# Row maxima a batch and a half ahead of the scores in two attention layers, and merged output rows in the first

## The chip, the cores and the metric

The kernel runs on one core of a Trainium2 chip. The metric is the device time of one execution in microseconds (us).

## The reference

A transformer block pair on 16 batches of 256 rows of 256 features, all float32, with a fixed context `ctx_1024` of the same shape. Attention has 16 heads of 16 features, the first one without projections, the second with them:

```python
x = x + attn0(layernorm(x), ctx, ctx)          # softmax(q k^T / 4) v, 16 heads
x = x + moe(layernorm(x))                      # 8 experts, top 2 of the gate's logits, gelu
x = x + attn1(ctx=ctx, q_in=layernorm(x))      # q = w_q x, k,v = w_kv ctx, softmax, w_out, b_out
x = x + ffn(layernorm(x))                      # relu, float_quantize to (4,3), second matmul
```

A layernorm is `(x - mean) / sqrt(var + 1e-5)` over the features. The softmax is over the 256 context rows of a batch.

## The kernel before, in words

Four phases follow one another: the first attention (about 0 to 289 us of the profiled span), routing and experts (to about 832 us), the second attention (to about 1150 us) and the last feed forward. The change touches only the two attentions, `first_attention` (L123 to L693) and `second_attention` (to L1568). Each engine has its own instruction stream, with a loop over bodies b, one for each batch and a few more at both ends, and within a body eight steps g, one for each pair of heads. All order is written out by hand: in each stream `body(b)` names the step g at which a piece of work stands, and for which batch (`has(b + k)` is true where that batch exists).

For a batch and a pair g the work is:

- **Row maximum**, M(g) below: TensorE multiplies 128 queries with 256 keys, four matmuls (`row_max`, L404), into a big PSUM bank. VectorE reduces it to the negated maximum of each row, R(g) below (`reduce`, L603), and this frees the bank. When all eight pairs are reduced, TensorE turns the maxima (`turn_neg`, L437), ScalarE copies them (`neg_out`, L547) and the SP queue writes them as one more row into `q_stack` (`stack_neg`, L270).
- **Score**, S(g) below: the same product the other way round, with the negated maximum in it (`score`, L415), into the next big bank. ScalarE takes the exponential (`exp`, L535), which frees the bank.
- **Probabilities by values**: `pv` (L428), 16 matmuls for four heads, into a spare bank, and `pv_out` on ScalarE (L541).
- **Output rows** of the batch before: TensorE turns them back (`out_rows`, L454), VectorE takes reciprocals of the row sums (L640) and multiplies (L644). In the first layer this is done in two halves q = 0 and 1, each in a spare bank; in the second layer (L1297, L1507, L1511) in one piece in a big bank. POOL adds the residual (`residual`, L345), VectorE takes statistics of the sum (`bn_stats` L608, `bn_aggr` L615, plus epsilon L617), POOL the power -1/2 (L331) and the normalised rows (L336). These are turned (L462) and multiplied with the gate weights (`logits`, L473, L651).
- **Queries and keys** of later batches: statistics at b + 4, normalised on POOL, turned for b + 3 (`turn_q`, L446), split into a high part (ScalarE, L553) and a low part (VectorE, `q_lo_out`, L634), and stacked by three DMAs each from the SP queue (`stack_q`, `stack_k`, L252). The second layer has projections in between (`project_q` L1274, `project_out` L1286) and gathers rows of the experts on POOL.

Two rings of PSUM banks set the order. The big ring has three banks, each two PSUM banks wide, the spare ring two. The n-th use of a ring takes bank n modulo its size, and waits until the use before in that bank has been read:

```python
for g in range(PAIRS):
    big_order += [(name, t) for name, t in ((("max", g), b + 2), (("score", g), b)) if has(t)]
spares, bigs = Ring(spare_order, 2), Ring(big_order, 3)
```

So with the order M, S, M, S, ... the score S(g + 1) takes the bank of M(g) and waits for R(g), and M(g + 1) takes the bank of S(g - 1) and waits for its exponential. In the code before the maxima are those of batch b + 2 while the scores are those of b. The first bodies, b = -2 and -1, have maxima only, the bodies 14 and 15 scores only.

Of the kernel before, what the change touches and what calls it, by code (L numbers as in the profile page):

```python
# [122 lines left out]
def first_attention(nc, const, dram, weights, raw, kvT, ctx_in, ctx_loaded):  # L123
    FIRST, END = -5, BATCHES + 2
    PARTS = 3 * 16
    MAX_ROW = STACK - 1
    LN_STEPS = 2 * QT + 1
    RAMP = 3
    spare_order, big_order = [], []
    for b in range(FIRST, END):  # L130
        spare_order += [(name, t) for name, t in (
            (("pv", 3), b - 1), ("negT", b + 1), ("qT", b + 3), (("out", 0), b - 1), (("out", 1), b - 1), (("pv", 0), b),
            ("normT", b - 2), (("pv", 1), b), ("logits", b - 2), (("pv", 2), b)) if has(t)]
        for g in range(PAIRS):
            big_order += [(name, t) for name, t in ((("max", g), b + 2), (("score", g), b)) if has(t)]
    spares, bigs = Ring(spare_order, 2), Ring(big_order, 3)

    with ExitStack() as ctx:
# [94 lines left out]
        def _(sp):  # L233
# [39 lines left out]
            def body(b):  # L273
                if has(b + 5):
                    load_x(b + 5)
                if has(b + 4):
                    load_k(b + 4)
                if has(b - 2):
                    sp.wait_ge(norm2_ready, (b - 1) * QT)
                    sp.dma_start(tiled(dram["norm2"], b - 2), norm2[b % 2][:]).then_inc(norm2_stored[b % 2], 16)  # L280
                if has(b + 3):
                    stack_k(b + 3)
                if has(b + 2):
                    load_v(b + 2)
                if has(b + 1):
                    stack_neg(b + 1)
# [31 lines left out]
        def _(pool):  # L318
# [10 lines left out]
            def power(veps, rs, ln_done, rs_ready, t):  # L329
                pool.wait_ge(ln_done, (t + 1) * LN_STEPS)  # L330
                nc.gpsimd.tensor_tensor(rs[:], veps[:], neg_half[:, 0:QT], ALU.pow).then_inc(rs_ready, 1)  # L331

            def apply(src, dst, rs, mv, rs_ready, done, t):
                pool.wait_ge(rs_ready, t + 1)
# [4 lines left out]
            def residual(d):  # L339
                if has(d - 2):  # L340
                    pool.wait_ge(stored[d % 2], d // 2 * 16)
                    pool.wait_ge(norm2_ready, (d - 1) * QT)
                for q in range(QT):
                    read_spare(pool, (("out", q), d))
# [21 lines left out]
            def body(b):  # L366
# [6 lines left out]
                if has(b + 3) and b + 3 >= RAMP:  # L373
                    split_k(b + 3)
                if has(b + 4):
                    power(var_eps, rstd, ln_step, rstd_ready, b + 4)
# [4 lines left out]
                if has(b - 1):  # L381
                    residual(b - 1)
# [3 lines left out]
                    power(var_epsb, rstdb, ln2_step, rstd2_ready, b - 1)  # L386
# [8 lines left out]
        def _(pe):  # L395
# [53 lines left out]
            def out_rows(d, q):  # L449
                for gg in range(GROUPS):  # L450
                    read_spare(pe, (("pv", gg), d))
                bank = free_spare(pe, (("out", q), d))
                for gg in range(GROUPS):
                    last = nc.tensor.transpose(spare[bank][:, gg * P:(gg + 1) * P], outT[d % 2][:, gg, q * P:(q + 1) * P], ident[:])  # L454
                last.then_inc(filled[bank], 1)
# [21 lines left out]
            def body(b):  # L477
                for g in range(PAIRS):
                    if has(b + 2):
                        row_max(b + 2, g)  # L480
                    if has(b):
                        score(b, g)
                    if g == 0:
                        if has(b - 1):
                            pv(b - 1, 3)
                        if has(b + 1):
                            turn_neg(b + 1)
                    elif g == 1:
                        if has(b + 3):
                            turn_q(b + 3)  # L490
                        if has(b - 1):
                            out_rows(b - 1, 0)
                    elif g == 2:
                        if has(b - 1):
                            out_rows(b - 1, 1)
# [3 lines left out]
                    elif g == 4:  # L499
                        if has(b - 2):  # L500
# [4 lines left out]
                    elif g == 6:  # L505
                        if has(b - 2):
                            logits(b - 2)
# [8 lines left out]
        def _(act):  # L516
# [20 lines left out]
            def pv_out(b, gg):  # L537
                if has(b - 2):
                    full_spare(act, (("out", 1), b - 2))
# [21 lines left out]
            def body(b):  # L561
                if has(b + 4) and b + 4 < 4:
                    clear_k(b + 4)
# [1794 lines left out]
```

## Time and profile before

| | before |
|---|---|
| median of 3 runs | 1277.8 us (1277.34 to 1283.1) |
| profiled execution: its own time, its span | 1278.05 us, 1276.3 us |
| TensorE busy | 1140.6 us, 89% |
| VectorE busy | 934.5 us, 73% |
| ScalarE busy | 739.0 us, 58% |
| POOL busy | 585.2 us, 46% |
| mean granted TensorE clock | 0.966 of 2.4 GHz |

The span runs from the first to the last instruction; 1.75 us of the execution lie around it. The shares are means over four phases with different limits, so the attentions have to be read by themselves.

### The profile page before, as it was taken

To read this page: it belongs to the slowest core of one execution; us is meant where nothing else is said; L and a number is where in the kernel's file an instruction comes from. 1 tells how busy PE (TensorE), PEld (TensorE's weight loads), DVE (VectorE), ACT (ScalarE), POOL (GpSimd) and SP (SyncE) were. 2 spreads that over 40 slices of the span, in tenths; PEclk is the share of its full clock that TensorE was granted. 3 is DMA by queue.
4 is the path that set the end of the run, shared out by engine and by line. 5 is a ranking of instruction groups with operands and counts; after the bars stand their busy time and mean duration, and the time that the engine had idled before them with its cause. 6 is when DMAs were issued, how large, how long until landed. Compare 5 with 4: busy or idle time off the path is not lost. (4 is left out here: it accounts for less than half of the span.)

```text
span 1276.3 us, 26854 instructions
## 1 busy us (share of the span) xinstructions
PE 1140.6 (89%) x9615; PEld 932.8 (73%) x9616; DVE 934.5 (73%) x1378; ACT 739.0 (58%) x978; POOL 585.2 (46%) x555
## 2 busy tenths in 40 slices
PE   3788999978879999999999999925898999999997
PEld 2455666548879999999999999814666666668886
DVE  7798999728548887887878877568788888843332
ACT  3376777766445665565455556233777777774443
POOL 1367776444458588653202000067777776201221
PEclk9999999998989999999999999956999999999999
DMA  5556766428963645563113111055566665411221
GB/s 189 191 192 200 242 209 236 146 92 281 344 218 119 203 148 172 170 201 107 41 49 107 41 49 41 26 200 171 195 217 214 204 201 194 165 44 44 79 73 45
DMA packets 120983, 193.41 MB, mean 152 GB/s; under 512 B 12160, under 2 KB 64384, under 8 KB 120768
## 3 DMA queue, kind: packets, MB, share of 16 engines
q1 hardware_dynamic: 95840, 140.71, 32.5%
q0 software_dynamic: 12576, 39.07, 9.9%
q10 hardware_dynamic: 12480, 12.47, 2.9%
q8 instruction: 55, 0.90, 0.3%
q14 instruction: 32, 0.26, 0.1%
HBM read 91.80 MB, written 49.55 MB: 111 GB/s over the span
## 5 line engine op out<-in xcount | busy, mean ns | idle before, releaser
L2128 PE MATMUL y_ps<-e_w,hiddenT_hi 128*128 x624 | 225.2, 404 | 1.6 <-DVE slot_y L2232 1.6
L2164 ACT ACTIVATE hidden<-hidden 128x1024 f32<-128x1024 f32 x78 | 82.8, 1062 | 186.2 <-DVE hidden L2197 186.2
L2111 PE MATMUL h_ps<-slot_xT_hi,tile_w_hi 128*128 128x256 f32 x624 | 178.1, 285 | 3.0 <-DVE slot_xT_lo L2215 3.0
L1458 DVE TENSOR_REDUCE neg_max<-big 128x4 fp32r<-128x1024 f32 x128 | 155.3, 1221 | 31.5 <-PE big L1215 29.8
L2111 PE MATMUL h_ps<-slot_xT_lo,tile_w_hi 128*128 128x256 f32 x624 | 177.8, 285 | 0.0
L2111 PE MATMUL h_ps<-slot_xT_hi,tile_w_lo 128*128 128x256 f32 x624 | 177.7, 285 | 0.0
L2129 PE MATMUL y_ps<-e_w,hiddenT_lo 128*128 x624 | 175.3, 281 | 0.0
L603 DVE TENSOR_REDUCE neg_max<-big 128x4 fp32r<-128x1024 f32 x128 | 155.2, 1222 | 21.2 <-PE big L404 18.8
L535 ACT ACTIVATE probs<-big 128x1024 f32<-128x1024 f32 x128 | 131.0, 1023 | 57.7 <-PE big L415 56.8
L1374 ACT ACTIVATE probs<-big 128x1024 f32<-128x1024 f32 x128 | 131.0, 1026 | 45.0 <-PE big L1226 44.8
L2221 DVE TENSOR_TENSOR hiddenT_lo<-hidden,hiddenT_hi 128x1024 fp32r<-128x1024 f32 x78 | 101.5, 1342 | 58.2 <-ACT hiddenT_hi L2175 58.2
L1136 POOL DMA_INDIRECT rows<-slots_out,slot x64 | 64.9, 1014 | 161.7 <-POOLq L1962 147.7
L2128 PEld LDWEIGHTS y_ps<-e_w,hiddenT_hi 128*128 128x128 f32 x624 | 117.4, 188 | 29.1 <-issue 2.0
L2111 PEld LDWEIGHTS h_ps<-slot_xT_hi,tile_w_hi 128*128 128x128 f32 x624 | 120.8, 194 | 5.4 <-DVE slot_xT_lo L2215 3.7
L2111 PEld LDWEIGHTS h_ps<-slot_xT_hi,tile_w_lo 128*128 128x128 f32 x624 | 120.9, 194 | 0.0
L2111 PEld LDWEIGHTS h_ps<-slot_xT_lo,tile_w_hi 128*128 128x128 f32 x624 | 120.9, 194 | 0.0
L2129 PEld LDWEIGHTS y_ps<-e_w,hiddenT_lo 128*128 128x128 f32 x624 | 118.3, 190 | 0.0
L2197 DVE TENSOR_TENSOR hidden<-h_ps,e_b1T 128x1024 f32<-128x1024 f32 x78 | 95.2, 1220 | 25.3 <-PE h_ps L2111 25.1
L2189 DVE TENSOR_TENSOR tile_w_lo<-e_w,tile_w_hi 128x1024 fp32r<-128x1024 f32 x76 | 103.9, 1367 | 9.8 <-issue 6.3
L1616 POOL DMA_INDIRECT staging<-norm,token_of_slot x76 | 95.5, 1256 | 30.6 <-issue 22.1
L1215 PE MATMUL big<-k_stack,q_stack 63*128 63x256 f32 x512 | 66.9, 345 | 27.0 <-DMA q_stack<-q_cut 14.4
L1215 PEld LDWEIGHTS big<-k_stack,q_stack 63*128 63x128 f32 x512 | 41.2, 200 | 61.9 <-issue 47.3
(238 smaller groups left out, 2600.3 us busy)
## 6 DMA issues: line engine op xcount, KB each, us to landing
k_stack<-k_cut SPq DMA_DIRECT2D x96, 256.0 KB, 3.9
q_stack<-q_cut SPq DMA_DIRECT2D x96, 256.0 KB, 3.0
e_w<-in_L_ffn_w POOLq DMA_DIRECT2D x10, 1024.0 KB, 5.9
slots_out<-slot_y ACTq DMA_DIRECT2D x39, 256.0 KB, 2.2
slots_in<-staging POOLq DMA_DIRECT2D x38, 256.0 KB, 2.7
slot_x<-slots_in SPq DMA_DIRECT2D x38, 256.0 KB, 2.8
vals<-in_v_wide SPq DMA_DIRECT2D x16, 512.0 KB, 4.1
v_wide<-v_out SPq DMA_DIRECT2D x16, 512.0 KB, 5.8
```

The costliest lines, as they stand in the source:

```text
L535: nc.scalar.activation(probs[g][:], big[bank][:], ACT.Exp, scale=SCALE).then_inc(big_freed[bank], 1)
L603: nc.vector.tensor_reduce(neg_max[m % 2][:, :, :, g].rearrange("p q a -> p a q").bitcast(F32R), big[bank][:], AX.X, ALU.max, negate=True). ...
L1215: last = nc.tensor.matmul(big[bank][:, par, q, :], q_stack[m % 4][rows, g, q * P:(q + 1) * P].bitcast(F32R), k_stack[m % 4][rows, g, :].bi ...
L1374: nc.scalar.activation(probs[g][:], big[bank][:], ACT.Exp, scale=SCALE).then_inc(big_freed[bank], 1)
L1458: nc.vector.tensor_reduce(neg_max[m % 2][:, :, :, g].rearrange("p q a -> p a q").bitcast(F32R), big[bank][:], AX.X, ALU.max, negate=True). ...
L1616: pool.indirect_dma_start(out=rows[:, q, :], out_offset=None, in_=dram["norm2"], in_offset=bass.IndirectOffsetOnAxis(ap=const["token"][:, ...
L2111: last = nc.tensor.matmul(h_ps[k][:, f % HF, :], w1[w][b.u][:, c, f * P:(f + 1) * P], xT[a][b.u][:, c, :], start=(n == 0), stop=(n == 3 * ...
L2128: nc.tensor.matmul(y_ps[q][:].rearrange("p s d -> p (s d)"), hT[0][o.u][:, f, rows], both, start=(f == 0), stop=False)
L2129: last = nc.tensor.matmul(y_ps[q][:, 0, :], hT[1][o.u][:, f, rows], both[:, 0:DIM], start=False, stop=(f == FC - 1))
L2189: nc.vector.tensor_tensor(w1[1][n.u][:, c, :], of_place(expert_w["w1"], c, places.of(n)), w1[0][n.u][:, c, :].bitcast(F32), ALU.subtract). ...
L2197: nc.vector.tensor_tensor(hidden[:, HF * k:HF * (k + 1), :], h_ps[k][:], bias.unsqueeze(2).to_broadcast([P, HF, SLOT_ROWS]), ALU.add).then ...
L2221: nc.vector.tensor_tensor(hT[1][b.u][:, half, :], hidden[:, half, :], hT[0][b.u][:, half, :].bitcast(F32), ALU.subtract).then_inc(hT_ready, 1)
```

## The change

In both layers the row maxima run 12 steps ahead of the scores instead of 16: at step g of body b stand the maxima `maxima(b, g)`, which is pair (g + 4) mod 8 of batch b + 1 for g < 4 and of b + 2 from g = 4 on. With them the turns of maxima, queries and keys, the clearing of stacks, the statistics and most users of spare banks move by four steps, on all streams. In the first layer the output rows become one use of a big bank, at step 2 on TensorE and step 3 on VectorE, with one reciprocal and one multiplication for both halves; epsilon is added by POOL ahead of the power; the logits of a batch come a body later. The SP queue's order changes: `stack_neg` goes ahead of `stack_k` in the first layer, the loads and stores are put first.

```diff
 def first_attention(...):
-    FIRST, END = -5, BATCHES + 2
+    FIRST, END = -5, BATCHES + 3
-    LN_STEPS = 2 * QT + 1
+    LN_STEPS = 2 * QT
+    OUT_AT = 2
+    HALF = PAIRS // 2
+    def maxima(b, g):
+        return divmod((b + 1) * PAIRS + g + HALF, PAIRS)
...
-            (("pv", 3), b - 1), ("negT", b + 1), ("qT", b + 3), (("out", 0), b - 1), (("out", 1), b - 1), (("pv", 0), b),
-            ("normT", b - 2), (("pv", 1), b), ("logits", b - 2), (("pv", 2), b)) if has(t)]
+            (("pv", 3), b - 1), ("logits", b - 3), (("pv", 0), b), ("negT", b + 1), ("normT", b - 2), (("pv", 1), b),
+            ("qT", b + 3), (("pv", 2), b)) if has(t)]
-            big_order += [(name, t) for name, t in ((("max", g), b + 2), (("score", g), b)) if has(t)]
+            m, gm = maxima(b, g)
+            big_order += [(name, t) for name, t in ((("max", gm), m), (("score", g), b), ("out" if g == OUT_AT else None, b - 1))
+                          if has(t) and name]
...
             def power(mv, veps, rs, ln_done, rs_ready, t):
                 pool.wait_ge(ln_done, (t + 1) * LN_STEPS)
+                nc.gpsimd.tensor_scalar(veps[:], mv[:, :, 1], EPS, None, ALU.add).then_inc(rs_ready, 1)
+                pool.wait_ge(rs_ready, 2 * t + 1)
                 nc.gpsimd.tensor_tensor(rs[:], veps[:], neg_half[:, 0:QT], ALU.pow).then_inc(rs_ready, 1)
...
             def body(b):                      # TensorE, new order
                 for g in range(PAIRS):
-                    if has(b + 2):
-                        row_max(b + 2, g)
+                    m, gm = maxima(b, g)
+                    if has(m):
+                        row_max(m, gm)
                     if has(b):
                         score(b, g)
...
+                    g == 0: pv(b - 1, 3);  1: logits(b - 3);  2: out_rows(b - 1);  3: pv(b, 0)
+                    g == 4: turn_neg(b + 1), turn_norm2(b - 2);  5: pv(b, 1);  6: turn_q(b + 3);  7: pv(b, 2)
...
-                dve.wait_ge(step, t * LN_STEPS + 2 * QT)
-                nc.vector.tensor_scalar(veps[:], mv[:, :, 1], EPS, None, ALU.add).then_inc(step, 1)
...
-            def out_rows(d, q):               # VectorE
-                bank = full_spare(dve, (("out", q), d))
+            def out_rows(d):
+                bank = full_big(dve, ("out", d))
+                nc.vector.reciprocal(recip[:], heads[:, :, :, DH]).then_inc(recip_done, 1)
+                nc.vector.tensor_tensor(att[d % 2][...], heads[:, :, :, 0:DH], recip[...], ALU.mult).then_inc(big_freed[bank], 1)
...
+            VectorE after R(g), g == 0, 1: nothing;  2: logits(b - 3);  3: out_rows(b - 1);  4: ln_stats(b + 4)
+            g == 5: ln_var(b + 4), ln_stats of y_out(b - 1);  6: q_lo_out(b + 3), ln_var of b - 1;  7: nothing
...
 def second_attention(...):
+            ("attT", b - 2), (("pv", 3), b - 1), ("oproj", b - 2), (("pv", 0), b), ("normT", b + 3), ("negT", b + 1),
+            (("pv", 1), b), ("qT", b + 3), (("pv", 2), b)) if has(t)]
...
+            TensorE: g == 0: turn_att(b - 2);  1: pv(b - 1, 3);  2: project_out(b - 2);  3: pv(b, 0)
+            g == 4: turn_norm(b + 3), out_rows(b - 1);  5: turn_neg(b + 1), pv(b, 1);  6: project_q(b + 3);  7: pv(b, 2)
```

The lines with `g ==` in this cut sum up `if` chains of the new code. On POOL the residual of b - 1 goes ahead of the power and the normalised rows of b + 4.

## Rows read from the trace of the kernel before

**Rows 1.** Windows: engine busy times (instruction counts), granted clock, DMA share, GB/s.
```profile
63.10:254.70 191.60, 174.37 (x1987) 115.39 (x1983) 172.87 (x300) 143.26 (x198) 122.94 (x132) 0.99 0.60 204
139.80:153.95 14.15, 13.18 (x155) 8.69 (x153) 13.28 (x25) 10.80 (x15) 9.62 (x10) 1.00 0.78 262
262.11:272.86 10.75, 10.26 (x119) 6.29 (x117) 2.71 (x10) 9.79 (x15) 4.95 (x6) 1.00 0.21 75
925.10:1092.40 167.30, 154.78 (x1707) 109.62 (x1711) 140.47 (x192) 126.79 (x197) 125.61 (x118) 1.00 0.60 200
1122.20:1132.80 10.60, 10.53 (x127) 6.76 (x120) 5.32 (x18) 9.15 (x15) 1.03 (x1) 1.00 0.24 80
```

**Rows 2.** Groups by line, 125 to 225 us, VectorE; busy us, mean ns; POOL whole span.
```profile
L603 DVE TENSOR_REDUCE neg_max<-big 128x4 fp32r<-128x1024 f32 x56 | 68.5, 1223 | 4.6 <-PE big L404 3.2
L644 DVE TENSOR_TENSOR att<-spare,recip 128x256 f32<-128x256 f32 x14 | 5.9, 424 | 0.5
L608 DVE BATCH_NORM_STATS2 stat6b<-y_out 128x6 f32<-128x256 f32 x14 | 5.2, 413 | 0.3 <-POOL y_out L345 0.3
L634 DVE TENSOR_TENSOR q_cut<-spare,q_cut 128x512 fp32r<-128x512 f32 x7 | 4.8, 689 | 0.4 <-ACT q_cut L553 0.2
L640 DVE RECIPROCAL recip<-spare 128x16 f32<-128x16 f32 x14 | 3.5, 247 | 0.0
L617 DVE TENSOR_SCALAR var_eps<-mean_var 128x2 f32<-128x2 f32 x7 | 2.5, 350 | 0.2
L617 DVE TENSOR_SCALAR var_epsb<-mean_varb 128x2 f32<-128x2 f32 x7 | 1.2, 169 | 0.2
L615 DVE BATCH_NORM_AGGREGATE mean_varb<-stat6b 128x2 f32<-128x6 f32 x14 | 1.7, 161 | 0.0
...
L331 POOL TENSOR_TENSOR rstd<-var_eps,neg_half 128x2 f32<-128x2 f32 x16 | 11.4, 713 | 51.0 <-DVE var_eps L617 50.3
```

**Rows 3.** Timeline in one body of the first layer: start us, us, engine, line [idle before].
```profile
145.33 2.54 DVE L603 TENSOR_REDUCE neg_max<-big 128x4 fp32r<-128x1024 f32 x2
...
146.61 0.50 PE L415 MATMUL big<-q_stack,k_stack 64*128 64x256 f32 x4
...
147.04 1.07 PE L428 MATMUL spare<-probs,vals 128*32 128x256 f32 x16
...
148.04 0.50 PE L404 MATMUL big<-k_stack,q_stack 63*128 63x256 f32 x4
...
148.71 1.06 PE L473 MATMUL spare<-gate_w,norm2T 128*128 128x8 f32 x8
...
149.70 0.50 PE L404 MATMUL big<-k_stack,q_stack 63*128 63x256 f32 x4
...
151.38 0.51 PE L404 MATMUL big<-k_stack,q_stack 63*128 63x256 f32 x4
...
151.99 1.23 DVE L603 TENSOR_REDUCE neg_max<-big 128x4 fp32r<-128x1024 f32 x1 [0.44 <-PE big L404]
```

**Rows 4.** Timeline of the second layer's merged output rows.
```profile
998.56 1.22 DVE L1458 TENSOR_REDUCE neg_max<-big 128x4 fp32r<-128x1024 f32 x1
...
998.57 1.09 PE L1297 MATMUL big<-ident,outT 128*128 128x128 f32 x8
...
999.70 0.36 DVE L1507 RECIPROCAL recip<-big 128x32 f32<-128x32 f32 x1
...
1000.09 0.69 DVE L1511 TENSOR_TENSOR att<-big,recip 128x512 f32<-128x512 f32 x1
```

**Rows 5.** Timeline of TensorE before the first score, and that score; first and second layer.
```profile
35.77 0.80 PE L404 MATMUL big<-k_stack,q_stack 63*128 63x256 f32 x4 [0.99 <-DVE neg_max L603]
...
42.47 0.79 PE L415 MATMUL big<-q_stack,k_stack 64*128 64x256 f32 x4 [0.33 <-DVE neg_max L603]
...
881.82 0.51 PE L1215 MATMUL big<-k_stack,q_stack 63*128 63x256 f32 x4 [0.53 <-DVE neg_max L1458]
...
888.68 0.65 PE L1226 MATMUL big<-q_stack,k_stack 64*128 64x256 f32 x4
```

More of the change, by code:

```diff
@@ L374, in body @@
                     split_k(b + 3)
+                if has(b - 1):
+                    residual(b - 1)
                 if has(b + 4):
-                    power(var_eps, rstd, ln_step, rstd_ready, b + 4)
+                    power(mean_var, var_eps, rstd, ln_step, rstd_ready, b + 4)
                 if has(b + 4) and b + 4 >= RAMP:
@@ L381, in body @@
                 if has(b - 1):
-                    residual(b - 1)
                     if has(b - 3):
@@ L447, in turn_q @@
                 last.then_inc(filled[bank], 1)
-            def out_rows(d, q):
+            def out_rows(d):
                 for gg in range(GROUPS):
                     read_spare(pe, (("pv", gg), d))
[L452 to L455, printed above, removed]
+                bank = free_big(pe, ("out", d))
+                for q in range(QT):
+                    for gg in range(GROUPS):
+                        last = nc.tensor.transpose(big[bank][:, q, gg // 2, gg % 2 * P:(gg % 2 + 1) * P], outT[d % 2][:, gg, q * P:(q + 1) * P], ident[:])
+                last.then_inc(big_filled[bank], 1)
             def turn_norm2(f):
@@ L505, in body @@
                     elif g == 6:
-                        if has(b - 2):
-                            logits(b - 2)
+                        if has(b + 3):
+                            turn_q(b + 3)
                     elif g == 7:
@@ L561, in body @@
             def body(b):
-                if has(b + 4) and b + 4 < 4:
-                    clear_k(b + 4)
-                if has(b + 3) and b + 3 < RAMP:
-                    k_hi_out(b + 3)
                 if b == 3:
@@ L576, in body @@
                 for g in range(PAIRS):
+                    if g == HALF and has(b + 4) and b + 4 < 4:
+                        clear_k(b + 4)
+                    if g == HALF and has(b + 3) and b + 3 < RAMP:
+                        k_hi_out(b + 3)
                     if has(b):
@@ L1301, in body @@
                 for g in range(PAIRS):
-                    if has(b + 2):
-                        row_max(b + 2, g)
+                    m, gm = maxima(b, g)
+                    if has(m):
+                        row_max(m, gm)
                     if has(b):
@@ L1408, in body @@
             def body(b):
-                if has(b + 3) and b + 3 < RAMP:
-                    k_hi_out(b + 3)
                 for g in range(PAIRS):
+                    if g == HALF and has(b + 3) and b + 3 < RAMP:
+                        k_hi_out(b + 3)
                     if has(b):
@@ L1450, in _, with clear_q @@
         def _(dve):
-            for u in range(4):
+            def clear_q(u):
                 nc.vector.memset(q_stack[u][:], 0.0).then_inc(q_zeroed, 1)
```

235 lines of the change are left out of this document (124 added, 111 removed).

## Prediction

> **What bounds the kernel now.** I read the windows first, for the attentions alone: the page's 89% and 73% are means over phases that the change doesn't touch. In 13 bodies of the first layer VectorE is busy 172.87 of 191.60 us and TensorE 174.37; a body takes 14.74 us on average and 14.15 in a quiet one, of which VectorE is busy 13.28 and TensorE 13.18 [rows 1]. Neither is idle for a whole microsecond in the quiet body, so it is tied by both engines and by how they hand banks to one another. Ten bodies of the second layer take 16.73 us each, and there TensorE (154.78 of 167.30) stands well ahead of VectorE (140.47) [rows 1]. Next the groups of VectorE, to see what it does beside eight reductions of 1.22 us [rows 2], and then the timeline, for the spacings of the hand-over. These carry the argument: a second reduction's bank is what the next score waits for, 146.61 - 145.33 = 1.28 us after a reduction began; score to next work 147.04 - 146.61 = 0.43 after a wait; a `pv` holds TensorE for 1.00 (147.04 to 148.04); maximum and score together 0.67 (148.04 to 148.71), half each; the gate's eight matmuls 0.99 (148.71 to 149.70); and a reduction that waited began 151.99 - 151.38 = 0.61 after its maximum [rows 3].
>
> **Part 1: less work for VectorE in the first layer.** Both epsilon operations go, 0.35 + 0.17 us a body. Two reciprocals and two multiplications, 2 x (0.25 + 0.42) = 1.34 [rows 2], become one of each at 0.36 + 0.69 = 1.05, which the second layer shows [rows 4]. Together 0.8 us a body less, from about 13.3 to 12.5. On POOL each epsilon costs more than nothing and not more than the power beside it, 0.71 [rows 2]; I take 0.3, nearer to the reciprocal's 0.25 on as few elements. POOL is busy 9.62 of 14.15 us [rows 1], so two of them fit inside a body; only in the chains at both ends of the layer do they lengthen the path, by 0.3 us in all (between nothing and 1.5 if three chains each pay a wake-up and 0.71 less the 0.17 saved).
>
> **Part 2: where the steps now stand in the first layer.** Saved work is time only if the hand-over doesn't open. It does. The big ring has three banks. With the output rows O taken after S(2), the uses run M2 S2 O M3 S3 M4 S4: M(3) takes the bank of M(2), S(3) that of S(2), and M(4) the bank of O. VectorE reads O after R(3), and its next instruction is R(4), which needs M(4), which needs O's bank. So between the multiplication and R(4) VectorE has nothing it may do: release 0.06 (1.28 less the reduction's 1.22), then 0.61. In the second layer before, O is used after S(4) and read in the same step, and M(5) had been there already.
>
> The second effect is how extras lie. TensorE's heavy steps are now 7, 0, 1, 2, 3 (1.00, 1.00, 0.99, 1.09, 1.00 us beside maximum and score), VectorE's are 3, 4, 5, 6, and it has nothing extra in 7, 0 and 1. TensorE can run at most one maximum ahead, because S(g + 1) waits for R(g). I lay one body out from R(6) = 0:
> - S(7) at 1.28, pv 1.71, M(0) 2.71. VectorE: reduction 1.14 (998.56 to 999.70 [rows 4]), low part of q 0.61 (0.69 less the 0.08 by which instructions overlap), two aggregates 0.3; R(7) 2.05, so S(0) not before 3.33.
> - pv 3.76, M(1) 4.76, logits 5.43, M(2) 6.42, out rows 7.09 to 8.18. R(2) begins at 6.42 + 0.61 = 7.03, so M(3) at 8.31 and R(3) at 8.92. VectorE by itself could have been there at about 6.8.
> - From R(3): reciprocal 1.14, multiplication 1.53, its end 2.22, M(4) 2.28, R(4) 2.89; statistics 0.75 (two of 0.41 less overlap); R(5) 4.78; aggregates 0.3 and statistics 0.75; R(6) 6.97.
>
> That makes 8.92 + 6.97 = 15.9 us for a body, bounded below by TensorE's and VectorE's own work with the bubble (12.5 + 0.67 = 13.2), above by this sum plus the three bodies that carry a weight copy on ScalarE, which would hide in the new idle time. The same laying out for the order of before gives 14.5, against 14.15 to 14.74 [rows 1], so I keep 15.9.
>
> **Part 3: the lead.** Maxima of half a batch less stand ahead of the first score. In the first layer the first score starts at 42.47, M(4) of batch 1 at 35.77 and takes 0.80 [rows 5]; with its maxima turned four steps earlier S(0) comes at about 36.6: 5.9 us earlier. In the second it comes from 888.68 to about 882.4, the end of the maximum at 881.82 [rows 5]: 6.3 us. The maximum that follows in the second layer waits for stacked queries and isn't earlier, so scores fill idle time there. At the other end half a body of scores alone (10.75 / 2 = 5.4, and 10.60 / 2 = 5.3 [rows 1]) goes, and half a full body comes in its place.
>
> **Part 4: the second layer's steps.** The same work on every engine. The chain from low part of q over its three DMAs to the first maximum spans six steps before and five and a half now; output rows still share a step with their reader. I find no stall that wasn't there, and take 16.73 us a body as before (between -0.5 and +1 us each, by TensorE's 12.5 idle in ten bodies below [rows 1] and by late maxima rows above, see the rivals). SP: `stack_neg` stands behind two loads whose conditions are long met, so it costs nothing while the maxima are turned four steps ahead of their score; if that cover goes, S(0) waits.
>
> **The sum**, against the profiled execution's own 1278.05 us (0.25 above the median of the runs). First layer: 13.5 x 15.9 - 191.60 = +23.1, less 5.4, less 5.9, plus 0.3: **+12.1**. Second: half of 16.73 is 8.4, less 5.3, less 6.3: **-3.2**. Together +8.9, so **1287 us**, 0.7% slower. A measurement of this kernel can tell about 0.5% (6.4 us) from no change.
>
> The Trainium skill, Perfetto Trace Analysis, section Identifying the Most-Contended Engine, says that the engine with the highest occupancy should be optimised first. By that rule the first layer, whose VectorE is over 90% busy, would gain what VectorE loses; it speaks for the first rival. The same page, Optimization Strategy, says that a gap that repeats on the engine that should be saturated can mean too little PSUM for the next tile; what I expect at R(4) is such a gap, and no row of before shows it.
>
> **The rivals.**
> 1. *VectorE's relief is paid out.* The gaps of the order don't add up, since the timeline reads only one body, and a body falls by 0.8 to 13.94. For: VectorE's 13.28 of 14.15 us. Against: TensorE is as full. First layer 13.5 x 13.94 - 191.6 = -3.4, less 11.3: -14.7; with -3.2: 1260 us. Chance 0.12.
> 2. *Relief and bubble cancel.* The 0.67 of R(4) eats the 0.8, TensorE's heavy steps are smoothed by waits that I counted twice. Body 14.74: +7.4 - 11.3 = -3.9, with -3.2: 1271 us. This decides the side: below 15.3 us a body the kernel is not slower (13.5 x 15.3 = 206.6, +15 against -14.5). Chance 0.2.
> 3. *Maxima rows land late in the second layer.* They are turned at step 5 behind eight steps before; one microsecond of wait at S(0) in 14 bodies adds 14 us: 1301. For: three steps of 2 us for copy, two DMA issues and landing. Chance 0.08.
> 4. *TensorE stays at its lower clock.* With 3 us idle a body instead of 1 it may be granted 1.2 GHz as in the ramp, where a maximum takes 0.80 instead of 0.50 [rows 5, 3]; all of TensorE's work then takes more, at least 0.3 x 8 us a body: over 1310. Chance 0.04.
> 5. *Nothing of it holds:* the change does what it says but other waits give the same times; within 1278 to 1284. Chance 0.12, shared by both neighbours.
>
> **How the numbers follow.** My own case has 0.44 and its range is 1281 to 1293 (a body of 15.5 to 16.3). Faster by over 0.5% (below 1271.7): rival 1 and half of rival 2, 0.22. Slower by over 0.5% (above 1284.4): my case without its lower edge, rivals 3 and 4 and a little of 5, 0.5. The rest, 0.28, within. The range has to reach to rival 2's middle and short of rival 3: 1268 to 1298.
>
> **What the profile will show.** If I am right: every body of the first layer is 15.5 to 16.3 us; R(4) of each waits some 0.7 us for TensorE's maximum right behind the merged multiplication; VectorE waits for maxima also at steps 0 to 3; TensorE waits for VectorE at M(4) over 1 us; VectorE busy in 100 us falls to about 80; first scores at 36 to 37 us; bodies of the second layer at 16.4 to 17. Wrong would be: a body under 15.3 us, no wait at R(4), or first scores later than 40 us, which would take part 3 away.

## The result, and the profile after

The kernel after takes 1295.38 us (median of 4 runs, 1290.51 to 1297.07) against 1277.8 us, a ratio of 1.0118 with a 95% interval of 1.0094 to 1.0142. It is slower, as forecast, by 17.6 us where 9 were forecast: inside the range of 1268 to 1298, above the 1281 to 1293 of the prediction's own case. Its profiled execution is the fastest of the four: 1290.51 us, with a span of 1288.8 us.

Windows of the kernel after: us, then busy time of TensorE, its weight load, VectorE, ScalarE and POOL, granted clock, DMA share and GB/s.

```profile
154.79:170.46 15.67, 13.67 (x156) 8.99 (x154) 12.71 (x21) 11.70 (x16) 10.30 (x13) 1.00 0.60 205
60.89:217.60 156.71, 135.31 (x1530) 88.55 (x1529) 127.09 (x200) 109.97 (x151) 109.39 (x132) 1.00 0.61 209
217.60:238.76 21.16, 15.50 (x157) 10.49 (x155) 12.73 (x21) 11.58 (x16) 10.30 (x13) 0.84 0.43 151
940.06:1106.80 166.74, 155.64 (x1716) 109.65 (x1707) 140.22 (x192) 129.23 (x198) 125.63 (x117) 1.00 0.61 201
```

The first two answer to the body and to the stretch of bodies in [rows 1]: ten bodies of the first layer in a row take 15.67 us each, and VectorE's share of them falls from over 90% to 81%. The third is the body that carries the first half of `w2T`: 21.16 us. The fourth is ten bodies of the second layer, 16.67 us each where they were 16.73.

Groups of VectorE and POOL in the kernel after, 125 to 225 us: busy us, mean ns, then idle time before them and what ended it. They answer to [rows 2].

```profile
L615 DVE TENSOR_REDUCE neg_max<-big 128x4 fp32r<-128x1024 f32 x52 | 62.7, 1217 | 16.2 <-PE big L416 16.2
L654 DVE TENSOR_TENSOR att<-big,recip 128x512 f32<-128x512 f32 x6 | 4.2, 692 | 0.2
L650 DVE RECIPROCAL recip<-big 128x32 f32<-128x32 f32 x6 | 2.1, 348 | 0.0
L340 POOL TENSOR_SCALAR var_epsb<-mean_varb 128x2 f32<-128x2 f32 x7 | 1.6, 232 | 0.0
```

The operations are as cheap as was reckoned (0.35 and 0.69 us; an epsilon 0.23 on POOL). But in 100 us the reductions now wait 16.2 us for a maximum of TensorE, where they waited 4.6 us, and only 52 of them fit where there were 56.

Timeline of VectorE in the kernel after, from R(5) of one body to R(4) of the next; columns: start, us, engine, line, operation, idle time before it.

```profile
156.57 1.21 DVE L615 TENSOR_REDUCE neg_max<-big 128x4 fp32r<-128x1024 f32 x1
...
160.68 2.33 DVE L615 TENSOR_REDUCE neg_max<-big 128x4 fp32r<-128x1024 f32 x2
164.00 1.23 DVE L615 TENSOR_REDUCE neg_max<-big 128x4 fp32r<-128x1024 f32 x1 [0.99 <-PE big L416]
165.66 1.23 DVE L615 TENSOR_REDUCE neg_max<-big 128x4 fp32r<-128x1024 f32 x1 [0.43 <-PE big L416]
166.80 0.17 DVE L661 TENSOR_TENSOR all_logits<-spare,gate_b 128x16 f32<-128x16 f32 x1
167.48 1.23 DVE L615 TENSOR_REDUCE neg_max<-big 128x4 fp32r<-128x1024 f32 x1 [0.52 <-PE big L416]
168.62 0.35 DVE L650 RECIPROCAL recip<-big 128x32 f32<-128x32 f32 x1
169.00 0.69 DVE L654 TENSOR_TENSOR att<-big,recip 128x512 f32<-128x512 f32 x1
170.46 1.23 DVE L615 TENSOR_REDUCE neg_max<-big 128x4 fp32r<-128x1024 f32 x1 [0.76 <-PE big L416]
```

And TensorE in the same body: the output rows, then M(3), S(3), the value product, and M(4), which waits for the bank that the multiplication gives back.

```profile
165.79 1.09 PE L467 MATMUL big<-ident,outT 128*128 128x128 f32 x8
166.94 0.50 PE L416 MATMUL big<-k_stack,q_stack 63*128 63x256 f32 x4
167.28 0.40 PE L427 MATMUL big<-q_stack,k_stack 64*128 64x256 f32 x4
167.60 1.07 PE L440 MATMUL spare<-probs,vals 128*32 128x256 f32 x16
169.84 0.51 PE L416 MATMUL big<-k_stack,q_stack 63*128 63x256 f32 x4 [1.17 <-DVE att L654]
```

Both engines stand still one behind the other: TensorE 1.17 us at M(4), until `att` is done, and then VectorE 0.76 us at R(4), until M(4) is there. VectorE also waits 0.99, 0.43 and 0.52 us at steps 1 to 3.

The first scores of both layers start at 37.04 and 896.35 us (the second 49.1 us after the first DMA that ScalarE gives out for the second layer, which was 56.6 before):

```profile
37.04 0.79 PE L427 MATMUL big<-q_stack,k_stack 64*128 64x256 f32 x4 [0.56 <-DVE neg_max L615]
...
896.35 0.62 PE L1241 MATMUL big<-q_stack,k_stack 64*128 64x256 f32 x4
```

Last, the long body, read from all engines' timeline:

```profile
225.28 0.60 SPq L300 DMA_DIRECT2D x<-y_out  x1
225.92 0.51 SPq L308 DMA_DIRECT2D raw<-in_f_w_T  x1
...
229.71 1.06 ACT L583 ACTIVATE w2T<-raw 128x1024 fp8e4<-128x1024 f32 x1 [5.18 <-DMA raw<-in_f_w_T]
231.74 0.50 PEld L416 LDWEIGHTS big<-k_stack,q_stack 63*128 63x128 f32 x4 [3.88 <-ACT probs L547]
231.74 0.80 PE L416 MATMUL big<-k_stack,q_stack 63*128 63x256 f32 x4 [3.79 <-ACT probs L547]
232.57 1.23 DVE L615 TENSOR_REDUCE neg_max<-big 128x4 fp32r<-128x1024 f32 x1 [4.58 <-PE big L416]
```

ScalarE waits 5.18 us for the raw weights. Behind it in its order stand the exponentials, behind them the banks: TensorE idles 3.79 us and VectorE 4.58. After that a maximum takes 0.80 us instead of 0.50; the mean granted clock from 231 to 237 us is 0.60:

```profile
231.00:237.00 6.00, 5.21 (x40) 3.84 (x40) 2.58 (x4) 3.81 (x5) 0.00 (x0) 0.60 0.14 53
```

The kernel before waited for the same load, but 1.25 us:

```profile
221.42 0.47 SPq L299 DMA_DIRECT2D raw<-in_f_w_T  x1
225.87 1.06 ACT L575 ACTIVATE w2T<-raw 128x1024 fp8e4<-128x1024 f32 x1 [1.25 <-DMA raw<-in_f_w_T]
```

SP gives the load out 4.45 us ahead of the copy there and 3.79 us ahead here. What changed is when SP gives it out, measured against when ScalarE is ready for it: before, ScalarE began to wait at 224.62 us, 3.20 us after the issue; here at 224.53 us, 1.39 us ahead of the issue at 225.92. The stacking of q and the store of x1 stand ahead of the load in SP's order, and they moved towards the end of the body, because q is turned at step 6 instead of 1.

**Where the 12.5 us between the two profiled executions lie.** The first layer ends (last addition of gate logits on VectorE) at 300.09 instead of 288.88 us: +11.2. The second layer and the feed forward behind it, from ScalarE's first computation there to the end, take 441.1 instead of 443.8: -2.7. What lies between them is the same code, and took 547.6 instead of 543.6: +4.0. This last one isn't the change's: in the eleven kernels below, which share this code, it took 544.7 to 552.4, 548.4 in the kernel whose first layer is that of before, and 548.9 in the one that differs from before by the epsilon alone. The trace of before has the shortest of all.

Within the first layer, by the spacing of ScalarE's copy of the maxima rows: 13 spacings go from 192.3 to 208.4 (+16.1), of which body 12 is 21.2 - 15.7 = 5.5 and the other 10.6 the general lengthening. The first two spacings and the tail behind the last one lose 1.5 and 3.3.

### The profile page after: what moved, and what is told of

Read it like the earlier page. It is cut to its first block and busy times, and to the rows that moved or that the text cites. A ratio compares the mean times of both kernels' runs of the same rounds, so it can differ in the third digit from the quotient of the medians.

```text
span 1288.8 us, 26776 instructions
## 1 busy us (share of the span) xinstructions
PE 1140.1 (88%) x9615; PEld 932.5 (72%) x9616; DVE 925.9 (72%) x1314; ACT 741.3 (58%) x978; POOL 592.7 (46%) x587
## 5 line engine op out<-in xcount | busy, mean ns | idle before, releaser
L2221 DVE TENSOR_TENSOR tile_w_lo<-e_w,tile_w_hi 128x1024 fp32r<-128x1024 f32 x76 | 106.6, 1402 | 13.2 <-issue 7.8
L2229 DVE TENSOR_TENSOR hidden<-h_ps,e_b1T 128x1024 f32<-128x1024 f32 x78 | 95.1, 1220 | 18.4 <-PE h_ps L2143 18.1
L1648 POOL DMA_INDIRECT staging<-norm,token_of_slot x76 | 91.8, 1208 | 32.1 <-issue 21.6
```

Source lines behind the costliest of these rows:

```text
L1648: pool.indirect_dma_start(out=rows[:, q, :], out_offset=None, in_=dram["norm2"], in_offset=bass.IndirectOffsetOnAxis(ap=const["token"][:, ...
L2221: nc.vector.tensor_tensor(w1[1][n.u][:, c, :], of_place(expert_w["w1"], c, places.of(n)), w1[0][n.u][:, c, :].bitcast(F32), ALU.subtract). ...
L2229: nc.vector.tensor_tensor(hidden[:, HF * k:HF * (k + 1), :], h_ps[k][:], bias.unsqueeze(2).to_broadcast([P, HF, SLOT_ROWS]), ALU.add).then ...
```

## The experiments

All eleven differ from the kernel after or before in the first or second layer alone. Ratios are against 23 runs of the kernel before on the same chip as each group of kernels, whose medians were 1280.3, 1278.64 and 1279.87 us; a difference between medians of two groups is therefore rougher than one between ratios. Every ratio holds what the second layer gives as well, except in the kernels whose second layer is that of before (before with an epsilon on POOL, and first layer only). "L1 end" is the end of the first layer as above; bodies are spacings of the maxima rows. The first four ran together, then the next four, then the last three.

| kernel | median us (runs) | ratio, 95% interval | L1 end | usual body | body 12 |
|---|---|---|---|---|---|
| before | 1277.8 (4) | 1 | 288.88 | 14.7 (mean) | 16.2 |
| after | 1295.38 (4) | 1.0118 (1.0094 to 1.0142) | 300.09 | 15.7 | 21.2 |
| second layer only | 1276.55 (12) | 0.9961 (0.9932 to 0.9989) | 288.36 | as before | as before |
| first layer only | 1299.18 (6) | 1.0149 (1.0126 to 1.0172) | 301.28 | 15.7 | 21.5 |
| raw weights early | 1287.77 (6) | 1.0059 (1.0036 to 1.0082) | 297.78 | 15.7 | 15.7 |
| rows read at step 2 | 1277.45 (12) | 0.9976 (0.9961 to 0.9991) | 285.77 | 14.6 | 21.6 |
| before, epsilon on POOL | 1279.57 (12) | 1.0014 (1.0001 to 1.0027) | 285.45 | 14.7 (mean) | 16.2 |
| after, epsilon on VectorE | 1298.03 (6) | 1.0144 (1.0116 to 1.0172) | 304.6 | 16.0 | 21.7 |
| statistics early | 1292.78 (6) | 1.0119 (1.0096 to 1.0142) | 302.08 | 15.6 | 21.4 |
| three edits | 1275.44 (12) | 0.9976 (0.9959 to 0.9993) | 282.56 | 14.6 | 18.4 |
| rows written at step 3 | 1293.99 (6) | 1.0124 (1.0099 to 1.0149) | 297.88 | 15.2 | 22.0 |
| rows split again | 1278.82 (12) | 0.9994 (0.9977 to 1.0011) | 288.3 | 15.0 | 20.4 |
| rows at step 2, raw at body 10 | 1270.68 (12) | 0.9941 (0.9925 to 0.9958) | 280.07 | 14.6 | 14.6 |

### Each layer by itself

Two kernels: one takes only `second_attention` from the kernel after, the other only `first_attention`. The expectations:

> The new second layer with the first layer of before. My theory (the first layer's new order costs, the second layer's lead pays): the second layer's part of the span falls by about 3 us, as in the changed kernel's profile (441.6 against 444.3 us), so about 1275 us, ratio 0.998. Rival (what was lost lies in the second layer or between the layers): ratio 1.003 or more, with the stretch between first and second layer 4 us longer than the 542.6 us of before.

> The new first layer with the second layer of before. My theory: the first layer ends about 11 us later, as in the changed kernel, and nothing is given back: 1290 to 1298 us, 2 to 3 us above the changed kernel at most. If the 4 us between the layers belong to the new first layer, they are here too: the stretch from the first layer's last logits to the second layer's first load is 546 us; if they are chance, it is 542 to 543. Rival: under 1285 us, the loss would then need both layers.

By the ratios the second layer's half of the change gains 5.0 us and the first layer's half loses 19. The first layer's half came out slower than expected: 1299.18 us, above the 1290 to 1298. In its trace the first layer ends 12.4 us later than in before's; the stretch between the layers, 548.5 us, is as long as in the kernel with the second layer's half alone, so the 4 us there don't belong to the new first layer. The loss is all in the first layer's half, which is where the steps of the prediction put it, and the second layer gains what the earlier first score gives: from there to the end it is 439.8 to 441.1 us wherever it has the new order, and 441.9, 443.8 and 445.0 where it has the old.

### The raw weights asked for a body earlier

```
-                elif b == 11:
+                elif b == 10:
                     sp.wait_ge(w_lo, 2)
                     sp.dma_start(raw[:], half_w2(dram["f_w2_T"], 0)).then_inc(w_loaded, 16)
```

> The changed kernel with the load of the first half of the last feed forward's second weights issued at the end of body 10 of the SP queue instead of 11. In the changed profile ScalarE waits 5.2 us for it at the start of body 12 and that body takes 21.2 instead of 15.7 us. Theory A (this wait is all on the path): body 12 takes 15.7 to 16.7, the time falls by 4.5 to 5.5 us against the changed kernel, ratio to before about 1.0075. Theory B (the wait is taken from slack that is used later): under 2 us.

The copy on ScalarE no longer waits, and the 21-us body is gone (its copy at 228.64 us lies within a spacing of 15.7):

```profile
214.56 0.48 SPq L308 DMA_DIRECT2D raw<-in_f_w_T  x1
...
228.64 1.05 ACT L583 ACTIVATE w2T<-raw 128x1024 fp8e4<-128x1024 f32 x1
```

The kernel is 7.6 us faster than after by medians, 7.5 by ratios: more than the 4.5 to 5.5 expected, though the ratio's interval reaches to them. In its one profiled execution the first layer is only 2.3 us shorter, since two other spacings took 17.1 us and one in the ramp 16.7. Its windows show what went with the two:

```profile
188.00:191.00 3.00, 2.94 (x28) 1.36 (x25) 3.00 (x8) 2.49 (x4) 0.57 (x2) 0.67 0.05 11
...
197.00:200.00 3.00, 3.00 (x41) 2.21 (x31) 1.57 (x3) 2.17 (x3) 2.91 (x4) 1.00 0.76 263
...
206.00:209.00 3.00, 3.00 (x24) 1.50 (x26) 2.44 (x7) 1.97 (x4) 0.94 (x2) 0.51 0.07 23
```

In two short stretches the granted clock is 0.67 and 0.51. Both lie ahead of the issue of the raw weights at 214.56 us, so these are falls of the clock and not a cost of the load.

### VectorE reads the output rows at step 2

```
                     elif g == 2:
                         if has(b - 3):
                             logits(b - 3)
-                    elif g == 3:
                         if has(b - 1):
                             out_rows(b - 1)
```

> The changed kernel with VectorE reading the merged output rows right after the reduction of step 2 instead of step 3, so that their bank is free before the maximum of step 4 wants it. Theory A (bank hand-over: 0.76 us of VectorE's wait at step 4 and 1.17 us of TensorE's behind it): the wait at step 4 goes, the wait of step 3 takes little, a body falls from 15.7 to 14.5 to 14.8 us, in 14 bodies 12 to 16 us: ratio to before 0.998 to 1.003. Theory B (only the uneven steps cost, the bubble is taken from slack): a body stays above 15.3 us and the ratio above 1.008.

This is the decisive one. Nothing is moved on TensorE, no work is added or removed, and VectorE reads the rows one reduction earlier. (That frees their bank sooner, and it also moves 1.05 us of VectorE's work from step 3 to step 2; the kernels with rows written at step 3 and with rows split again, below, take these apart in part.) Its timeline:

```profile
158.06 1.23 DVE L615 TENSOR_REDUCE neg_max<-big 128x4 fp32r<-128x1024 f32 x1 [0.43 <-PE big L416]
159.20 0.17 DVE L661 TENSOR_TENSOR all_logits<-spare,gate_b 128x16 f32<-128x16 f32 x1
159.32 0.36 DVE L650 RECIPROCAL recip<-big 128x32 f32<-128x32 f32 x1
159.71 0.69 DVE L654 TENSOR_TENSOR att<-big,recip 128x512 f32<-128x512 f32 x1
160.32 2.53 DVE L615 TENSOR_REDUCE neg_max<-big 128x4 fp32r<-128x1024 f32 x2
```

R(3) follows the multiplication at once and R(4) follows R(3) (one row for the two, 2.53 us); TensorE doesn't wait for `att` at all in 125 to 200 us, where after waits 4.7 us in four times. The waits at steps 1 and 2 stay, 1.00 and 0.43 us, so they aren't the rows' doing. Bodies fall by 1.1 us to 14.6, the first layer by 14.3 us, and the kernel by 17.9 us in the medians, a little more than the 12 to 16 expected. The second layer's 5.0 us are in its ratio of 0.9976, so this first layer alone isn't shown to be better than that of before. Body 12 keeps its wait, 6.07 us here.

### Epsilon alone, in both orders

The first kernel is before with the epsilons of the first layer on POOL; the second is after with them back on VectorE.

```
             def power(mv, veps, rs, ln_done, rs_ready, t):
                 pool.wait_ge(ln_done, (t + 1) * LN_STEPS)
+                nc.gpsimd.tensor_scalar(veps[:], mv[:, :, 1], EPS, None, ALU.add).then_inc(rs_ready, 1)
+                pool.wait_ge(rs_ready, 2 * t + 1)
...
```

> The kernel before, with only the epsilon of the first layer moved from VectorE to GpSimd; order, lead and output rows as before. Theory (VectorE and TensorE hand three banks to and fro, and each other's work lies in the hand-over, so that less VectorE work alone pays little): L1 ends 0 to 3 us earlier than 288.9, ratio 0.997 to 1.001. Rival (VectorE is the bound of the first layer, and what is taken from it is gained in full): two epsilons of some 0.2 us a body, with their waits 0.4 us, over 16 bodies 6 to 7 us, ratio 0.995 or below.

> The kernel after, with only the epsilon put back on VectorE in the first layer (steps 5 and 6 of a body). Theory: both epsilons lie on the chain of bank hand-overs in steps 5 and 6, so bodies grow from 15.7 to 15.9 to 16.1, the first layer by 3 to 6 us, ratio about 1.015. Rival (VectorE's work is no longer in the way, the loss of the change is TensorE waiting for the merged output rows alone): bodies stay at 15.7 and the ratio at 1.012.

In the order of before the epsilon is worth nothing that could be measured: 1.0014, just above the 0.997 to 1.001 expected, and eight spacings from the copy at 120.66 to that at 238.56 take 14.74 us each, against 14.69 (124.60 to 242.11) in before:

```profile
120.66 0.36 ACT L549 ACTIVATE neg_rows<-spare 16x256 f32<-16x256 f32 x1
...
238.56 0.36 ACT L549 ACTIVATE neg_rows<-spare 16x256 f32<-16x256 f32 x1
```

(The first layer as a whole ends 3.4 us earlier than in before's trace; one ramp body and one with a lower clock are shorter, and the medians say that nothing is gained.) In the order of after it is worth 0.3 us a body, some 4 us of the first layer; the medians differ by 2.7 us, which their intervals don't tell from 4 or from nothing. That fits steps 4 to 6 of VectorE lying on the path there and not in before, which is argued and not shown. The expectation of bodies of 15.9 to 16.1 us held. For the order of before the rival that VectorE's relief is paid out as such has fallen: its 0.5% isn't there.

### The statistics of the next tile at steps 0 and 1

`ln_stats` and `ln_var` of batch b + 4, for b from 0 on, moved from steps 4 and 5 to steps 0 and 1 of VectorE; the rows stay at step 3.

```
                     if g == 0:
+                        if has(b + 4) and b >= 0:
+                            dve.wait_ge(ln_step, (b + 4) * LN_STEPS)
+                            dve.wait_ge(x_loaded[b % 2], ((b + 4) // 2 + 1) * 16)
+                            ln_stats(x_in[(b + 4) % 8], stat6, ln_step)
+                    elif g == 1:
+                        if has(b + 4) and b >= 0:
+                            ln_var(stat6, mean_var, ln_step, normed_ready, b + 4)
...
```

> The kernel after, with the statistics of the next input tile (bn_stats and bn_aggr of batch b+4) taken from steps 4 and 5 on VectorE, where the merged output rows have just delayed it, to steps 0 and 1, where it waits; the rows themselves stay at step 3. Theory (the wait of R(4) for the score banks and the wait of M(4) for att set the body, the order of the rest only its tail): bodies 15.2 to 15.4, first layer 4 to 8 us shorter than after, ratio 1.006 to 1.009. Rival (uneven filling of the steps, too much at 3 to 6 and nothing at 0 to 2, is the whole cause): bodies at 14.7 and below, ratio 1.000 or below. Body 12 keeps its wait for the raw weights in both, about 21.

Neither the theory's number nor the rival's came out: bodies went from 15.67 to 15.6 instead of 15.2 to 15.4, and the time not at all; the first layer ends 2.0 us later, with three spacings of 16.7 to 17.1 in the ramp. The wait of M(4) for `att` is there as before, and what was taken out between R(4) and R(5) comes back: VectorE waits 0.56 us instead of 0.23 for ScalarE's part of q, and the next body's S(0) 0.67 us for R(7) instead of 0.34, so that it starts 164.83 - 157.08 = 7.75 us after M(4) where it was 162.02 - 154.16 = 7.86:

```profile
157.08 0.50 PE L416 MATMUL big<-k_stack,q_stack 63*128 63x256 f32 x4 [1.17 <-DVE att L654]
164.83 0.50 PE L427 MATMUL big<-q_stack,k_stack 64*128 64x256 f32 x4 [0.67 <-DVE neg_max L615]
```

So filling the idle steps with this work is worth next to nothing. Other pieces of VectorE's work weren't moved, and none of TensorE's for this question.

### Three edits together

Rows read at step 2, statistics at steps 0 and 1, and the raw weights asked for in body 11 ahead of the stacking of q instead of behind it:

```
+                if b == 11:
+                    sp.wait_ge(w_lo, 2)
+                    sp.dma_start(raw[:], half_w2(dram["f_w2_T"], 0)).then_inc(w_loaded, 16)
                 if has(b + 3):
                     stack_q(b + 3)
```

> The kernel after with three edits in the first layer: VectorE reads the merged output rows at step 2, where TensorE writes them, the statistics of batch b+4 at steps 0 and 1, and the raw weights of body 12 asked for in body 11 before the stacking of q and the store of x1. Theory: bodies 14.2 to 14.5, body 12 at 15 to 17 instead of 21.6, first layer ends at 274 to 282, ratio 0.985 to 0.995, below both kernels. Rival (the load of the raw weights costs about 3 us wherever it is put, and the statistics are hidden at step 4 now that the rows are gone): no better than the rows at step 2 alone, 0.9976.

All four numbers of the theory were missed, two of them narrowly (bodies and the end of the first layer). Bodies are those of the rows alone, 14.6. Body 12 comes down only to 18.4, as the load is still late:

```profile
211.34 0.60 SPq L298 DMA_DIRECT2D raw<-in_f_w_T  x1
216.14 1.06 ACT L583 ACTIVATE w2T<-raw 128x1024 fp8e4<-128x1024 f32 x1 [3.90 <-DMA raw<-in_f_w_T]
```

The copy starts 4.80 us after the issue, in after 3.79 and in before 4.45; ScalarE was ready for it 0.90 us after the issue, so this place in SP's order is too close to the copy to hide the load. By its ratio of 0.9976 this kernel is no better than the rows alone, which speaks for the rival in the small; its first layer is 3.2 us shorter.

### Rows written at step 3

TensorE writes the output rows at step 3, behind S(3) and ahead of the value product, and VectorE reads them at step 3 as in after.

```
-    OUT_AT = 2
+    OUT_AT = 3
...
                     elif g == OUT_AT:
                         if has(b - 1):
                             out_rows(b - 1)
-                    elif g == 3:
                         if has(b):
                             pv(b, 0)
```

> The kernel after, with TensorE writing the merged output rows at step 3 instead of 2 (behind score 3, ahead of the first value product); VectorE reads them at step 3 as in after, so that they hold their score bank for no step in between. Theory (what costs is the bank held from step 2 to step 3, one of three): bodies 14.6 to 15.0 instead of 15.7, the idle time of TensorE at M(4) that ends with att under 0.5 us, ratio 0.998 to 1.004. Rival (what costs is VectorE's reading of the rows at step 3, behind which the reduction of step 4 and TensorE wait, wherever they were written): bodies 15.5 or more, ratio 1.010 or above.

Half of it. TensorE's wait for `att` is gone, but the bodies are 15.2, between the two expectations, and the time (1.0124) is the rival's. VectorE has a new wait instead, for the rows themselves:

```profile
168.08 1.22 DVE L614 TENSOR_REDUCE neg_max<-big 128x4 fp32r<-128x1024 f32 x1
169.70 0.36 DVE L649 RECIPROCAL recip<-big 128x32 f32<-128x32 f32 x1 [0.40 <-PE big L467]
170.09 0.69 DVE L653 TENSOR_TENSOR att<-big,recip 128x512 f32<-128x512 f32 x1
171.20 1.23 DVE L614 TENSOR_REDUCE neg_max<-big 128x4 fp32r<-128x1024 f32 x1 [0.42 <-PE big L416]
```

0.40 + 0.42 us stand where 0.76 stood. The rows must be both written early enough not to be waited for and read at once; written at step 2 and read at step 2 is that place here. The profiled execution also has three spacings of 16.8 to 16.9, in each of which the granted clock is at 0.5, the lower of its two levels, for some 3 us, as in the kernel with early raw weights. The other executions seem to have such stretches too: the mean granted clock is 0.956 to 0.958 in all six, where the four of after have 0.959 to 0.962. That goes with a time no better than that of after in spite of shorter bodies; what makes the clock fall more often in this order isn't shown.

### The merge undone

Two halves in the spare banks again, written at steps 1 and 2 and read at steps 2 and 3; gate logits read at step 1. Everything else as in after.

```
-        (("pv", 3), b - 1), ("logits", b - 3), (("pv", 0), b), ...
+        (("pv", 3), b - 1), ("logits", b - 3), (("out", 0), b - 1), (("out", 1), b - 1), (("pv", 0), b), ...
```

> The kernel after, with the merge of the output rows undone alone: two halves in the spare banks, written at steps 1 and 2 and read at steps 2 and 3 as before; lead of a batch and a half, order of SP's queue and epsilon on GpSimd as in after. The first layer has about 0.5 us a body more work on VectorE. Theory (the lead and the rest are harmless, the merged rows in a score bank are the loss): bodies 14.3 to 14.8, body 12 at 20 to 22, L1 ends at 282 to 287, ratio 0.994 to 0.999. Rival (the lead's order or the two more operations cost as much as the bank): bodies 15.3 or more, ratio 1.006 or above.

The kernel is back at the time of before, and bodies fall by 0.7 us: the merged rows in a score bank, read a step late, are the greater part of what lengthened them. It isn't the whole: bodies are 15.0 rather than the 14.8 that I gave as the upper end, the first layer ends at 288.3 rather than 287, and body 12 keeps its wait of 5.21 us, so SP's new order does harm here as well. The second layer's 5.0 us hide this in the ratio: 0.9994 stands against 0.9961 of the kernel with the second layer's half alone. Merged rows read in time (14.6) are 0.4 us a body better than split ones.

### The version that beats both

Rows read at step 2, and raw weights at the end of body 10: the two edits whose diffs stand above.

> The kernel after with two edits in the first layer: VectorE reads the merged output rows at step 2, and the raw weights of body 12 are asked for at the end of body 10. Theory: body 12 falls from 21.6 to 15 to 17, the others stay at 14.6, the first layer ends at 279 to 282, ratio 0.992 to 0.996. Rival (lower TensorE clock or crowded transfers take it back): ratio 0.997 or above.

1270.68 us, ratio 0.9941: faster than the kernel before by 0.6%, some 7.5 us, and than the kernel after by some 23 us, both by the ratios. Most of the 7.5 is the second layer's: its half alone has 0.9961 (0.9932 to 0.9989), and the two intervals overlap, so the runs don't show that this first layer beats that of before. In the traces it ends at 280.07 us against 285.5 to 288.9 in the three kernels with the old order. Its spacings are 14.6 us from the fourth to the last but one, body 12 among them. Body 12 came out under the 15 to 17 us expected. The copy doesn't wait, and TensorE is busy 13.55 us of each 14.56:

```profile
120.99:237.46 116.47, 108.41 (x1238) 71.83 (x1236) 100.63 (x156) 88.07 (x124) 79.29 (x91) 1.00 0.64 217
...
201.48 0.48 SPq L308 DMA_DIRECT2D raw<-in_f_w_T  x1
...
213.81 1.05 ACT L583 ACTIVATE w2T<-raw 128x1024 fp8e4<-128x1024 f32 x1
```

## Why the prediction was right, and where it fell short

**Part 1, less work for VectorE: right as work, and rightly not booked as time.** Multiplication and reciprocal cost what the second layer had shown, the epsilon 0.23 us on POOL where I took 0.3. The trial of the epsilon alone in the old order shows that 0.5 us of such work is worth nothing measurable there; that both engines are full and tied by three banks is my reading of it. (The bound of 1.5 us for POOL at both ends doesn't add up: three times 0.71 - 0.17 is 1.6 before any wake-up. The 0.3 us that the sum takes for it wasn't measured by itself.)

**Part 2, the hand-over: right, in place and in size.** The gap at R(4) is 0.76 us (forecast 0.67), TensorE's wait at M(4) 1.17 (forecast over 1), the body 15.67 (forecast 15.9, range 15.5 to 16.3), and VectorE waits at steps 1 to 3, though not at step 0 as forecast. Piece by piece, R(6) to R(3) took 9.00 us (forecast 8.92) and R(3) to the next R(6) 6.67 (forecast 6.97). Reading the rows one step earlier takes away both waits and 1.1 us of each body: that is shown. Of this, not holding the bank over a step gives 0.4 us (rows written at step 3, 15.2), so the place of VectorE's reading counts beside the bank. The second effect that I named, heavy steps of TensorE against heavy steps of VectorE, was tried in one piece only: moving the statistics changed next to nothing. VectorE's waits at steps 1 and 2, 1.4 us together, stay with the rows read at step 2, and what sets them wasn't tried.

**The step that failed**, in a prediction whose direction and main mechanism held, is the clause "the three bodies that carry a weight copy on ScalarE, which would hide in the new idle time". The copies themselves do; the first half of `w2T` doesn't, because its load is given out behind the stacking of q and the store of x1 in SP's order, and these had moved towards the end of the body with the turning of q. The prediction follows SP's order for `stack_neg` in the second layer alone, and not up to this load, which occurs in one body only. It cost 5.5 us in body 12, the lower clock behind it (0.60 from 231 to 237 us) included, and it is the greater part of the 8.7 us by which the forecast fell short: the kernel that asks for it early is 7.6 us faster than after.

**Parts 3 and 4: right.** First scores at 37.04 us (forecast 36 to 37), in the second layer 7.5 us earlier (forecast 6.3); bodies there 16.67. The second layer gained 2.7 us in the traces (forecast 3.2), and the kernel with this half alone 5.0 us by its ratio and 3.8 between medians.

**The sum.** In the traces the first layer is +11.2 for a forecast of +12.1, but made up otherwise. 13 bodies give +10.6 (by my 15.9 they would have given 13 x 15.9 - 191.6 = +15.1), body 12 another +5.5, head and tail -4.9 where my terms left -3.0. Part of the last is a body of 19.3 us in before's ramp, outside of the stretch that I had read, which is 15.4 in after. Errors of both signs cancel here, and that the first layer's total came out so near in the traces is luck in part; by the runs its half of the change costs 19 us. The rest of the 17.6 us between the medians is beyond the traces: the profiled execution of after is 4.9 us below its median, and only one was profiled. I take short stretches at a lower clock for a part of it, as several of the traces show them, but this is an argument and wasn't shown.

**The rivals.** The sums of the first two leave out the 0.3 us for POOL that my own case adds; it changes neither. The first (relief paid out, a body of 13.94) is refuted by bodies of 15.67, and by the epsilon alone for the order of before. The second (cancel, a body of 14.74) didn't occur either. Its number is nearly reached once the rows are read at step 2, 14.6, but there without the gap that it set against the relief. The third (maxima rows late in the second layer) didn't occur. The fourth (lower clock throughout) didn't either: ten bodies in a row ran at 1.00 in spite of 2.1 us of idle TensorE in each; but single stretches at the lower level did occur.

## What to carry to other kernels

Ask of each buffer of a short ring how long it is held, and who needs that bank next. Held over one step, it stopped first the producer and then the consumer here: reading it one step sooner was worth 1.1 us a body, and taking 0.5 us of work off the busy engine nothing in the order of before and 0.3 us a body in the order of after. Writing and reading in one step isn't enough by itself: at step 3 it left bodies at 15.2, since the reader then waited for the rows. When a change has two halves, measure each alone, or the gain of one hides the loss of the other in every later ratio. When a step is moved within a body, follow its queue also to what stands behind it in single bodies only, weight loads above all; ask for such loads a whole body ahead of their reader.

## What was not expected of the hardware

- The reader of the load of 0.5 MB of raw weights started 3.8 to 4.8 us after SP gave it out in each of the eleven kernels in which it waited (3.79 in after, 4.45 in before, 4.50 with rows read at step 2, 4.80 with three edits), so that a few tenths in SP's order matter little and a body's distance settles it.
- In all eight kernels in which ScalarE waited 3.9 us or more for the raw weights of body 12, TensorE idled 2.17 to 4.56 us, and the granted clock then stood at 0.5 for 3 to 10 us. Where the load came in time or ScalarE waited 1.25 us at most, no such fall followed in four kernels of five.
- Beside these the granted clock falls in stretches of some 3 to 7 us at no fixed body: in the kernel with early raw weights at 189 and 206 us, in the one with rows written at step 3 at 103, 120 and 137 us, in before at 113 us. A body with such a stretch is 1.3 to 1.6 us longer. The one in before followed 1.51 us of idle time of TensorE, the others named no gap longer than the 0.8 to 1.2 us that every body of theirs has, and which most bodies have without a fall.
- The order of after and the ones derived from it run like clockwork, nine spacings in a row of 15.7 us, while those of before vary from 14.1 to 16.3 us. A mean over bodies of before hides this, and a single quiet body, such as I read, is 0.6 us better than the mean (14.15 and 14.74 [rows 1]).
